# Dividing the probabilities of both heads of a pair by their sums in one step on VectorE

## The reference

```python
x = LN(x)
q, k, v = einsum('bsd,hde->bhse', x, Wq / Wk / Wv)          # 16 heads of 64
scores  = where(causal, q @ k.T / sqrt(64), -inf)           # 256 x 256 a head
attn    = softmax(scores, axis=-1)                          # <- the step of the change
heads   = (attn @ v) laid side by side                      # 256 x 1024
y       = LN(x + heads @ Wo) * gamma + beta
x       = x + LN(y)
# then: router (top 2 of 8), expert of 128 -> 512 -> 128 with gelu, weighted sum, LN, residual
```

## Time and profile before

| | before |
|---|---|
| median of three runs | 799.53 us |
| the profiled execution | 799.0 us, span 797.2 us |
| TensorE busy | 740.3 us, 93% |
| VectorE busy | 622.0 us, 78% |
| ScalarE busy | 525.8 us, 66% |
| GpSimd busy | 267.0 us, 33% |
| granted TensorE clock, mean | 0.988 |

### The profile page before, as it was taken

How to read it: one execution, slowest core, us unless ns; L and a number is a source line. 1 busy time by engine, 2 the same in 40 slices (tenths; PEclk the granted TensorE clock), 3 DMA queues, 4 the chain that set the end, 5 groups by cost and what they waited for, 6 DMA issues and landing times.

```text
span 797.2 us, 19170 instructions
## 1 busy us (share of the span) xinstructions
PE 740.3 (93%) x5936; PEld 609.6 (76%) x5937; DVE 622.0 (78%) x2357; ACT 525.8 (66%) x1739; POOL 267.0 (33%) x397
## 2 busy tenths in 40 slices
PE   4999999999999999999999999999878889999964
PEld 3777777887878788888878888888757778888831
DVE  3668898988888898888889888888868665555526
ACT  4677777878777777777777777777645534444415
POOL 3005434133231413223131323323125644444425
PEclk9999999999999999999999999999989999999988
DMA  8420000000000000000000000000011322222156
GB/s 180 150 55 9 8 8 22 14 22 18 12 21 8 22 14 22 16 14 23 7 21 16 21 12 18 22 1 22 2 41 49 85 76 61 61 60 60 55 152 181
DMA packets 51623, 33.14 MB, mean 42 GB/s; under 512 B 10960, under 2 KB 48336, under 8 KB 51536
## 3 DMA queue, kind: packets, MB, share of 16 engines
q1 hardware_dynamic: 46608, 22.73, 11.0%
q0 software_dynamic: 4352, 9.05, 3.2%
q10 hardware_dynamic: 576, 0.27, 0.1%
HBM read 19.81 MB, written 12.22 MB: 40 GB/s over the span
## 4 chain that ended last, share of the span: by engine, by line
PE 82%; DVE 6%; ACT 4%; issue 3%; DMA 2%; DVEq 1%; SPq 0%; ACTq 0%; POOL 0%; POOLq 0%
PE PT1O L411 12%; PE SC L397 9%; PE A L417 6%; PE M L376 6%; PE M L378 5%; PE M L377 5%; PE SC L403 5%; PE PT L581 4%; PE A L592 3%; PE SC L592 3%; PE SC L400 3%; PE PT L424 3%; PE PT L425 3%; PE PT1O L428 3%; PE SC L376 2%
## 5 line engine op out<-in xcount | busy, mean ns | idle before, releaser
L1064 ACT ACTIVATE qk<-M 128x512 f32<-128x512 f32 x128 | 76.6, 598 | 138.6 <-PE M L378 138.6
L1070 ACT ACTIVATE prob<-SC,nmax 128x256 f32<-128x256 f32 x256 | 126.1, 492 | 0.0
L411 PE MATMUL PT1O<-pT,v_sb 128*64 128x256 f32 (+1 forms) x1024 | 112.2, 339 | 12.4 <-issue 7.6
L702 DVE TENSOR_SCALAR prob<-prob,rden 128x256 f32<-128x256 f32 x256 | 101.8, 398 | 9.0
L411 PEld LDWEIGHTS PT1O<-pT,v_sb 128*64 128x64 f32 x1024 | 65.7, 136 | 55.2 <-issue 22.6
L1277 POOL DMA_INDIRECT expert_rows<-v_sb,got x72 | 69.5, 965 | 83.4 <-ACT v_sb L1153 78.3
L1068 ACT ACTIVATE prob<-SC,nmax 128x128 f32<-128x128 f32 x256 | 97.0, 379 | 0.0
L397 PE MATMUL SC<-qk 64*128 64x256 f32 x512 | 91.0, 432 | 0.8 <-ACT qk L1064 0.8
L1008 DVE COPY hidT<-PT 128x512 f32<-128x512 f32 x72 | 49.7, 691 | 50.2 <-PE PT L581 48.4
L1270 POOL DMA_INDIRECT sent_rows<-rec,slot x64 | 63.6, 994 | 72.6 <-DVE slot L858 54.5
L1146 ACT ACTIVATE hid<-SC 128x512 f32<-128x512 f32 x72 | 43.1, 599 | 66.8 <-PE SC L378 64.1
(11 more groups left out here) (182 smaller groups left out, 1843.4 us busy)
## 6 DMA issues: line engine op xcount, KB each, us to landing
got<-sent_rows SPq DMA_DIRECT2D x72, 66.0 KB, 1.9
w_in<-expert_rows SPq DMA_DIRECT2D x16, 256.0 KB, 4.1
x_in<-L_attn_x SPq DMA_DIRECT2D x16, 128.0 KB, 2.1
w_in<-L_ffn_w SPq DMA_DIRECT2D x1, 2048.0 KB, 12.7
x_res<-L_attn_x SPq DMA_DIRECT2D x16, 128.0 KB, 2.1
w_sb<-L_ffn_w SPq DMA_DIRECT2D x8, 256.0 KB, 4.6
out<-y_out SPq DMA_DIRECT2D x8, 256.0 KB, 2.4
expert_rows<-v_sb,got POOLq DMA_INDIRECT x72, 2.3
```

The source lines that it names most:

```text
L411: last = mm(O[k * E:(k + 1) * E, cols], v_sb[:, t, h * E:(h + 1) * E], src[:, k, :], start=(t == 0), stop=(t == 1), skip_group_check=True)
L702: v.tensor_scalar(prob[:, par, k, P:3 * P], prob[:, par, k, P:3 * P], rden[:, par, k:k + 1], None, ALU.mult)
L1070: a.activation(prob[:, par, k, P:3 * P], SC[par][:, k, LATE_Q], ACT.Exp, bias=nmax[:, par, k:k + 1], accum_out=den[:, par, k:k + 1]).then_ ...
```

## The change

The reciprocals of all four sums of a pair are taken at once, after the last exponential of head 1, and the late parts of both heads are multiplied in one operation, the early parts in another. A tensor_scalar has only one value a partition for all its columns, so the two multiplications become tensor_tensor operations: their second operand is `rden`, spread over the columns of each head with a stride of zero. `prob`, `nmax`, `den` and `rden` get shapes in which the two heads lie one behind the other. `nrm` counts pairs in place of heads, and nothing on VectorE waits for `exp_done[0]` any more. The exponentials, the maxima and the transposes work on the same bytes in the same order as before.

```diff
...
@@ -523,7 +523,7 @@
                         qk_proj((j + 2) % NP)
 
                     if there(b):
-                        pe.wait_ge(nrm, 2 * p + 2)
+                        pe.wait_ge(nrm, p + 1)
                         if not (first and j == 0):
                             pe.wait_ge(pt0_sb, p)
                             pe.wait_ge(pt1_sb, p)
@@ -692,17 +692,18 @@
 
             def maxima(p, par):
                 dve.wait_ge(s_mm, p + 1)
-                v.tensor_reduce(nmax[:, par, 2:4], SC[par][:, :, EARLY_Q], AX_X, ALU.max, negate=True)
-                v.tensor_reduce(nmax[:, par, 0:2], SC[par][:, :, LATE_Q], AX_X, ALU.max, negate=True).then_inc(mx, 1)
-
-            def normalise_head(p, par, k):
-                dve.wait_ge(exp_done[k], p + 1)
-                v.reciprocal(rden[:, par, k:4:2], den[:, par, k:4:2]).then_inc(rc, 1)
-                dve.wait_ge(rc, 2 * p + k + 1)
-                v.tensor_scalar(prob[:, par, k, P:3 * P], prob[:, par, k, P:3 * P], rden[:, par, k:k + 1], None,
-                                ALU.mult)
-                v.tensor_scalar(prob[:, par, k, 0:P], prob[:, par, k, 0:P], rden[:, par, 2 + k:3 + k], None,
-                                ALU.mult).then_inc(nrm, 1)
+                v.tensor_reduce(nmax[:, par, 1, :], SC[par][:, :, EARLY_Q], AX_X, ALU.max, negate=True)
+                v.tensor_reduce(nmax[:, par, 0, :], SC[par][:, :, LATE_Q], AX_X, ALU.max, negate=True).then_inc(mx, 1)
+
+            def normalise_pair(p, par):
+
+                dve.wait_ge(exp_done[1], p + 1)
+                v.reciprocal(rden[:, par], den[:, par]).then_inc(rc, 1)
+                dve.wait_ge(rc, p + 1)
+                v.tensor_tensor(prob[:, par, :, 1:3, :], prob[:, par, :, 1:3, :],
+                                rden[:, par, 0, :].unsqueeze(2).unsqueeze(3).broadcast_to([P, 2, 2, P]), ALU.mult)
+                v.tensor_tensor(prob[:, par, :, 0, :], prob[:, par, :, 0, :],
+                                rden[:, par, 1, :].unsqueeze(2).broadcast_to([P, 2, P]), ALU.mult).then_inc(nrm, 1)
 
             def pT1_copy(p):
                 dve.wait_ge(t1_mm, p + 1)
@@ -740,8 +741,7 @@
                         if j == 6:
                             finish(b - 1)
                     if there(b):
-                        normalise_head(p, par, 0)
-                        normalise_head(p, par, 1)
+                        normalise_pair(p, par)
                         if j < NP - 1 or there(b, -1):
                             maxima(p + 1, (j + 1) % 2)
                     if isinstance(b, int) and b == 0 and j == 0:
...
```

More of the change, by code:

```diff
@@ L100, in sandwich_kernel @@
         v_sb = sb("v_sb", [P, T, H * E])
[L101 to L104, removed]
+        prob = sb("prob", [P, 2, 2, 3, P])
+        nmax = sb("nmax", [P, 2, 2, 2])
+        den = sb("den", [P, 2, 2, 2])
+        rden = sb("rden", [P, 2, 2, 2])
         pT0 = sb("pT0", [P, 2, S])
@@ L423, in p_transpose @@
                 for k in range(2):
-                    nc.tensor.transpose(PT0[:, k * S:k * S + P], prob[:, par, k, 0:P], ident[:])
-                    last = nc.tensor.transpose(PT0[:, k * S + P:(k + 1) * S], prob[:, par, k, P:2 * P], ident[:])
+                    nc.tensor.transpose(PT0[:, k * S:k * S + P], prob[:, par, k, 0, :], ident[:])
+                    last = nc.tensor.transpose(PT0[:, k * S + P:(k + 1) * S], prob[:, par, k, 1, :], ident[:])
                 last.then_inc(t0_mm, 1)
                 for k in range(2):
-                    last = nc.tensor.transpose(PT1[:, k * P:(k + 1) * P], prob[:, par, k, 2 * P:3 * P], ident[:])
+                    last = nc.tensor.transpose(PT1[:, k * P:(k + 1) * P], prob[:, par, k, 2, :], ident[:])
                 last.then_inc(t1_mm, 1)
@@ L1067, in exps @@
                 act.wait_ge(mx, p + 1)
[L1068 to L1071, removed]
+                a.activation(prob[:, par, k, 0, :], SC[par][:, k, EARLY_Q], ACT.Exp,
+                             bias=nmax[:, par, 1, k:k + 1], accum_out=den[:, par, 1, k:k + 1])
+                a.activation(prob[:, par, k, 1:3, :].rearrange("p n t -> p (n t)"), SC[par][:, k, LATE_Q], ACT.Exp,
+                             bias=nmax[:, par, 0, k:k + 1], accum_out=den[:, par, 0, k:k + 1]).then_inc(exp_done[k], 1)
             def pT0_copy(p):
```

## The result

The changed kernel takes 807.77 us (median of four runs, 806.26 to 808.97), the kernel before 799.07 us (four runs). The ratio is 1.0106, 95% interval 1.0076 to 1.0135: slower by 8.7 us. Forecast were 808.6 us and 9.1 us. The profiled execution took 806.26 us, its span is 804.5 us. The two profiled executions lie 7.3 us apart, the medians 8.7.

What follows compares the result with a forecast made beforehand. TensorE, almost without gaps, was taken to bound the attention, so its waits add time. 7.3 + 1.3 + 0.5 = 9.1 us on 799.0 gave 808.1, plus 0.5 for the median 808.6 us; range 801 to 816 us.

Steps and rivals of the forecast that it cites:

- The course of the division: On VectorE, from the last exponential to the division's end: 1.36 us, 0.49 us more than before; next instruction after 1.28 us.
- Pair 2: In a regular batch: transposes don't wait, but the next maxima start 0.33 us late, delaying TensorE by 0.23 us before L411.
- Pairs 4 and 5: In a regular batch: next maxima 0.11 and 0.38 us late; 0.38 us in all reaches TensorE by way of pT1_copy.
- Pairs 3, 6, 0, 1 and 7: In a regular batch: nothing added, through room of 0.2 to 0.4 us or TensorE's delay from earlier pairs.
- A regular batch: Each of the twelve batches 3 to 14: 0.61 us lost, 7.3 us in all.
- Batches 0 to 2 and 15: Batches where steps of earlier batches are partly missing: 1.3 us lost together, apart from GpSimd's splitting of weights.
- Pair 5 of batch 0: Largest loss outside the regular batches: the next instruction at 43.85 in place of 43.36, 0.49 us.
- The last batch: Batch 15: gets nearly 0.2 us back at each of pairs 4 and 7, where VectorE itself is late.
- rival (b): Faster, about 797 us: VectorE's load counts, and five of the 11 TensorE waits (8.1 us) vanish, -2 us; chance 0.08.
- the 0.5 us for GpSimd: Batches 1 and 2, beside GpSimd's splitting of weights: +0.5 us for the waits there, between -2 and +3.6 us.
- (a): Hidden or nearly so, 799.5 to 801.5 us: the new multiplications go at tensor_scalar's rate, course 1.09 us; chance 0.14.
- (c): Much slower, 815 to 820 us: course of 1.62 us, or GpSimd holds it up in most batches; chance 0.18.

## Why the prediction was right, and where not

The course of the division was right to 0.01 us: 1.36 us from the last exponential to the end, 1.28 to the next instruction, and the rates of the tensor_tensor (0.69 and 0.42 us where nothing disturbs them) are those of the rows of other lines. That it starts after the last exponential and needs 0.49 us longer behind it is what costs; the four tensor_scalar with the same end cost the same in the same slots. The path was right too: the loss reaches TensorE through pT1_copy and L411, and moving one step out of that path took away two thirds of the loss in slot 3.

Pair 2: 0.23 us forecast, 0.21 measured. Pairs 4 and 5: 0.38 forecast, 0.10 and 0.26 measured. Pairs 3, 6, 0, 1 and 7: nothing forecast, 0.02 us or less measured. A regular batch 0.61 against 0.57; twelve 7.3 against 7.0 us.

Batches 0 to 2 and 15: 1.8 us forecast with GpSimd's part, 1.7 measured (0.71, 0.80, -0.05 and 0.22 us). Pair 5 of batch 0 was the one with a row, at 0.49 us: 0.18 and 0.31 us came behind pairs 4 and 5 there. The last batch was to get something back in two places: it did, 0.17 us from pair 4 to 5 and 0.24 from 6 to 7, and lost 0.63 in others. That the sum fits is in part luck, since its parts were estimates. So is the median, off by 0.8 us: the forecast was built on the profiled execution, and there it said 9.1 us more where 7.3 were measured. The attention took 8.65 us more and its start 0.3, and the scatter behind it took 1.6 off.

Three things were wrong. VectorE's busy time was forecast near 567 us and is 587.5. I had added up durations, but a busy time counts overlapping instructions once, and six operations in a row overlap more often, by some 0.08 us each, than three. That makes 15 of the 20 us: the sum of all durations fell by 50 us, the overlap by 15. The other 5 us are longer durations (L703 0.710 on average, for 0.69, and the reciprocal of four sums 0.177, for 0.16). TensorE's idle time was to grow by 9 us and grew by 6.2 (56.9 to 63.1 us): its busy time rose by 1.1 us, and the part after the attention was 1.6 us shorter. And the earlier trace rows were misread: that answer adds TensorE's and its weight loading's idle time before the same transposes. The waits are 5.0 us in seven places for the loading and 3.2 us in four of these for the matmuls, not 8.1 us in eleven. Two things in the forecast hung on it: rival (b), which becomes weaker by it, and the bounds of the 0.5 us for GpSimd. Read rightly, the waits of batches 1 and 2 are 2.1 us for the loading in five places, and 0.8 us for the matmuls in two of them. They neither vanished nor grew by 0.7 us each; after the change they are 2.7 us in seven places.

Of the rivals, (a) and (c) fell with the rate of the tensor_tensor, (b) with VectorE's 34.5 us that bought nothing. The rule of the Trainium skill on the count of operations ("VectorE: DVE Perf Modes", Rules for kernel authors) holds for VectorE's load, which fell by these 34.5 us, and said nothing about the time of this kernel. The same row of the Trainium skill says not to fuse chained operations for performance, which the prediction left out; here the fused form was the slower one. The rule of the Trainium skill on GpSimd and a tensor_tensor ("SBUF — State Buffer", Who interferes with whom) is borne out: L703 took 1.11 us beside L1265.

## What to carry to other kernels

Fusing work over two producers saves instructions and moves all of it behind the later producer; ask how long the consumer's side takes from the last producer's end, before and after, and what stands in the same queue behind it. Follow the delay past the first consumer: here the transposes had room and the copy two steps later had none. And look into each gap of an in-order queue: here steps of 0.7 us stood in gaps of 0.3 us, ahead of a copy for which TensorE waits, and putting that right gained 0.4 us a batch, where the division with fewer operations gained nothing.

## What the runs showed of the hardware

In these rows two elementwise instructions of VectorE and GpSimd that read SBUF didn't share but queued: 1.11 in place of 0.69 us for 512 columns, 0.74 in place of 0.17 us for four columns. The ends tell it: the tensor_tensor of 512 columns ended 0.56 us behind GpSimd's instruction, the tensor_scalar of 256 columns 0.15 us, the one of four 0.02 us. That is close to what the columns alone take by an estimate from the rows of other sizes (0.53 us for 512 by 0.69 and 0.425 us, 0.14 us for 256 by 0.35 and 0.28 us), so the columns seem to wait for GpSimd's end and the fixed part not. Beside pT1_copy, which reads PSUM, the same instruction of GpSimd cost nothing: the copy took 0.42 us as ever.

In six of the fourteen traces, of six different kernels, the changed one (in one of its two traces) and the kernel in the better order among them, slot 1 of batch 0 is 1.6 to 1.8 us longer. Neither trace of the kernel before shows it. The rows are from the kernel with the better order: the first product by v behind TensorE's wait, and the busy times between 20 and 30 us, with the granted clock third from the end:

```profile
24.52 1.38 PE L411 MATMUL PT1O<-pT,v_sb 128*64 128x256 f32 x8 [1.89 <-ACT v_sb L1091]
```

```profile
20.00:30.00 10.00, 8.08 (x46) 6.35 (x46) 5.79 (x18) 4.78 (x15) 0.91 (x2) 0.83 0.21 82
```

In the first trace of the kernel before the same group lasted 0.87 us behind a wait of 1.71 us, and the granted clock of that stretch was 1.00. With 0.83 TensorE ran part of it at the 1.2 GHz level in place of 2.4. The length of the wait doesn't settle which execution gets it: in five of the six it was 1.88 to 1.94 us, but in the sixth (four tensor_scalar for the pair) 1.71 us, as in the eight traces with 1.00. The cause stays open; it is a reason not to read single spans to better than 2 us.
